# A new order for the prologue of a fused vision-transformer block, and for the first image's gates and weight mixing in its feed-forward phase

## The reference, cut to what matters

```python
h = tok(x, W, b, cls)                       # (4, 3137, 128)
h = h + attn(layernorm(h), ...)
h = h + ffn(layernorm(h), ...)
# attn: q, k, v = causal 4-tap convolutions of linear maps, silu, q and k normalised
#   S_t = a_t (S - b_t (S k_t) k_t^T) + b_t v_t k_t^T ;  o_t = S_t q_t
#   out = linear(zero-centred rms norm(o) * silu(linear(x)))
# ffn: gh = relu(x W^T + b) ; g = (gh gfc2^T + b2).mean(tokens)     # 8 gates per image
#   W1m = W1 + sum_e g_e tv_W1[e] ; W2m = W2 + sum_e g_e tv_W2[e]   # b1m, b2m alike
#   out = layernorm(x + relu(x W1m^T + b1m) W2m^T + b2m) * lng + lnb
```

## Time and profile before

| | |
|---|---|
| median of 3 runs | 855.02 us (854.75 to 856.34) |
| the profiled execution: time, span | 857.75 us, 855.8 us |
| mean granted TensorE clock | 0.992 |
| TensorE, VectorE, ScalarE, GpSimd busy | 95%, 76%, 58%, 43% of the span |
| instructions | 31627 |

### The profile page before, as it was taken

One profiled execution on the slowest core, in us unless ns is written; L12 is line 12 of the kernel. 1 busy time (PEld: TensorE's weight loads), 2 busy tenths in 40 slices (PEclk: granted clock), 3 DMA queues, 4 the chain that ended last, 5 costly groups with the idle time before them and its releaser, 6 DMA issues. The chain is left out here.

```text
span 855.8 us, 31627 instructions
## 1 busy us (share of the span) xinstructions
PE 817.1 (95%) x12064; PEld 643.9 (75%) x12064; DVE 646.8 (76%) x2313; ACT 500.3 (58%) x1773; POOL 364.8 (43%) x530
## 2 busy tenths in 40 slices
PE   7679999999999999999999999999999899999996
PEld 5457778787787788787787787777787577777775
DVE  4356888888888888888888888888784867777444
ACT  1335566666565666666665666666645366666664
POOL 3122332333333332333323333333311388888875
PEclk9989999999999999999999999999999999999999
DMA  2000122221122111111101111111012133333331
GB/s 59 16 12 13 47 61 50 62 62 50 45 58 54 33 32 31 38 38 34 36 25 38 33 25 37 38 32 32 28 53 74 34 113 119 118 112 111 111 111 44
DMA packets 78660, 45.35 MB, mean 53 GB/s; under 512 B 20357, under 2 KB 69803, under 8 KB 78511
## 3 DMA queue, kind: packets, MB, share of 16 engines
q1 hardware_dynamic: 77663, 42.80, 17.9%
q10 hardware_dynamic: 848, 0.54, 0.3%
HBM read 23.69 MB, written 19.63 MB: 51 GB/s over the span
## 5 line engine op out<-in xcount | busy, mean ns | idle before, releaser
L1952 ACT ACTIVATE work<-bank,b1mix 128x512 f32<-128x512 f32 x96 | 66.0, 688 | 63.5 <-PE bank L2047 63.4
L2073 PEld LDWEIGHTS bank<-work 128*128 128x128 f32 x768 | 89.7, 192 | 11.8 <-issue 11.8
L2047 PE MATMUL bank<-work 128*128 128x512 f32 x192 | 88.3, 602 | 3.2 <-DVE work L1827 3.2
L2073 PE MATMUL bank<-work 128*128 128x128 f32 x768 | 89.6, 275 | 0.0
L491 ACT ACTIVATE work<-bank 128x512 f32<-128x512 f32 x50 | 29.9, 598 | 98.3 <-PE bank L1330 98.3
L740 POOL TENSOR_SCALAR var2e<-mv 128x4 f32<-128x4 f32 x22 | 5.0, 229 | 167.0 <-DVE mv L946 167.0
L1329 PE MATMUL bank<-SA,work 128*128 128x256 f32 x200 | 69.5, 430 | 0.0
L2047 PEld LDWEIGHTS bank<-work 128*128 128x128 f32 x192 | 35.1, 193 | 38.7 <-issue 34.5
L1330 PE MATMUL bank<-SB,work 128*128 128x256 f32 x200 | 61.1, 388 | 0.0
L1280 PEld LDWEIGHTS bank<-work 32*32 32x32 f32 x3200 | 35.1, 107 | 32.9 <-issue 27.3
L1869 DVE TENSOR_TENSOR work<-bank,work 128x512 f32<-128x512 f32 x24 | 16.6, 692 | 55.6 <-PE bank L2073 55.6
(11 more groups left out here) (288 smaller groups left out, 2373.3 us busy)
## 6 DMA issues: line engine op xcount, KB each, us to landing
hn_kept<-work SPq DMA_DIRECT2D x25, 256.0 KB, 2.5
hnT_kept<-work SPq DMA_DIRECT2D x25, 256.0 KB, 2.3
work<-hnT_kept SPq DMA_DIRECT2D x25, 256.0 KB, 2.8
work<-hn_kept SPq DMA_DIRECT2D x25, 256.0 KB, 3.1
out_dram<-work SPq DMA_DIRECT2D x24, 256.0 KB, 2.5
tv<-in_L_ffn_tv_W_dram SPq DMA_DIRECT2D x16, 256.0 KB
work<-r_kept SPq DMA_DIRECT2D x25, 98.0 KB
work<-in_x_dram SPq DMA_DIRECT2D x23, 102.0 KB
```

Of the source, the lines that this page charges most:

```text
L1952: ins = nc.scalar.activation(hid[f][:, :], ps[:, :], ACT.Relu, bias=b1mix[:, of[0], f:f + 1])
L2047: ins = mm(ps[:, :], w1T[of[0]][:, f, :], ghT[par][:, :, :].rearrange("p t c -> p (t c)"), start=True, stop=True)
L2073: ins = mm(by4(bank[2 + par])[:, t, :], hid[f][:, t * C:(t + 1) * C], w2T[of[t]][:, f, :], start=(f == 0 and t == 0), stop=(f == FB - 1), ...
```

## The change

In the first pass the embedding now stands ahead of all constant products: it is followed by the transpose of the centred weights, the three tap products and four products of ones (`transpose_weights`), then the factor's transpose, then the folding products and twelve products of ones. VectorE copies the folded weights between statistics and their aggregation, does the output weights and masks and the folding in other places, with a last part (`fold_rest`) behind the pixel product. ScalarE's copies of the taps and gates follow the factor row. The thirteen loads follow the row's loads. In the second pass the factor row and the key columns come ahead of the queries, the query rows go to the end, with six products of ones behind them. The third pass gets products of ones at four places. In the feed-forward phase the first image's gates are made first, with a release of their own, the others' after four mixing steps; GpSimd's shift of the residual goes ahead, its bias additions go behind the last mixing step; the b2 products go between the first two and last two hidden products of the first unit. The helper functions in the second pass hold the code that stood there before; where they are only moved, the diff below leaves them out.

```diff
-        WARM = 8
+        WARM = 11
...
-            ffn["load"](sp)
...
+                if j == first:
+                    ffn["load"](sp)
...
-            act.wait_ge(taps_ps, 1)
-            for t, i in ((cwA, 0), (cwB, 4), (cbs, 2)):
-                ins = nc.scalar.copy(t, bank[i][:, 0:384])
-            ins.then_inc(taps_kept, 1)
-            act.wait_ge(gate_ps, 1)
-            nc.scalar.copy(SA[0:64, 256:386], bank[6][0:64, 0:130]).then_inc(gate_kept, 1)
+
+            def folded_parts():
+                act.wait_ge(taps_ps, 1)
+                for t, i in ((cwA, 0), (cwB, 4), (cbs, 2)):
+                    ins = nc.scalar.copy(t, bank[i][:, 0:384])
+                ins.then_inc(taps_kept, 1)
+                act.wait_ge(gate_ps, 1)
+                nc.scalar.copy(SA[0:64, 256:386], bank[6][0:64, 0:130]).then_inc(gate_kept, 1)
...
+                fill = j == first + 1
+                if fill:
+                    factor_row()
+                    keys_out()
+                    key_squares_and_queries()
+                else:
+                    key_squares_and_queries()
+                    factor_row()
+                    if j == first:
+                        folded_parts()
+                    query_squares()
+                    keys_out()
...
+                if fill:
+                    query_squares()
...
+                ffn["scalar_early"](act)
...
-                dve.wait_ge(pro_dve, 3)
+
+            def fold_rest():
+                kv, q = bank[5][:, 0:256], bank[5][:, 256:384]
+                dve.wait_ge(pro_dve, 4)
                 nc.vector.tensor_tensor(SA[:, 0:256], cbs[:, 0:256], SA[:, 0:256], ALU.add)
                 nc.vector.tensor_tensor(SB[:, 0:256], cwB[:, 0:256], kv, ALU.mult)
-                dve.wait_ge(pro_dve, 4)
+                dve.wait_ge(pro_dve, 5)
                 nc.vector.tensor_tensor(SA[:, 386:514], cbs[:, 256:384], SA[:, 386:514], ALU.add)
                 nc.vector.tensor_tensor(SB[:, 384:512], cwB[:, 256:384], q, ALU.mult).then_inc(folded, 1)
...
-                dve.wait_ge(pro_dve, 5)
+                dve.wait_ge(pro_dve, 3)
...
                     ins.then_inc(stats1_done, 1)
                     if s > 0:
                         keep_h0()
+                    else:
+                        fold_weights()
                     dve.wait_ge(stats1_done, s + 1)
                     need(dve, var1e_ready, s)
                     for b in range(NB):
                         ins = nc.vector.bn_aggr(mv1[:, b, :], stats1[:, b, :])
                     ins.then_inc(mv1_ready, 1)
                     if s == 0:
-                        fold_weights()
                         keep_h0()
-                        fold_taps()
                         output_weights()
...
+                if j != first + 1:
+                    key_factors()
...
+                if j == first + 1:
+                    key_factors()
...
                 if j == first:
-                    sub_masks()
+                    fold_taps()
...
+                if j == first:
+                    fold_rest()
+                    sub_masks()
...
-            pe.wait_ge(con, 2)
-            pe.wait_ge(taps_in, 16 * len(conv_taps))
-            mm(bank[0][:, 0:384], selA, cwT, start=True, stop=True)
-            mm(bank[4][:, 0:384], selB, cwT, start=True, stop=True)
-            mm(bank[2][:, 0:384], onehot1, cb_row[:, 0:384], start=True, stop=True).then_inc(taps_ps, 1)
             pe.wait_ge(we_in, 16 * len(embedding))
 
-            def fold_weights():
+            def keep_busy(n, at=7):
+
+                for _ in range(n):
+                    mm(bank[at][:, 0:D], ones[:, :], ones[:, :], start=True, stop=True)
+
+            def transpose_weights():
+                pe.wait_ge(con, 2)
                 pe.wait_ge(zeroed, 1)
                 pe.wait_ge(Wc_ready, 1)
                 tr(bank[3][:, 0:D], Wc, ident[:, :]).then_inc(WcT_ps, 1)
+                pe.wait_ge(taps_in, 16 * len(conv_taps))
+                mm(bank[0][:, 0:384], selA, cwT, start=True, stop=True)
+                mm(bank[4][:, 0:384], selB, cwT, start=True, stop=True)
+                mm(bank[2][:, 0:384], onehot1, cb_row[:, 0:384], start=True, stop=True).then_inc(taps_ps, 1)
+                keep_busy(4)
+
+            def fold_weights():
                 pe.wait_ge(WcT_ready, 1)
                 pe.wait_ge(proj_in, 16 * len(projection))
                 for to, at, n in ((0, 0, 256), (256, 384, 128)):
@@ -1261,6 +1304,8 @@
                     mm(bank[6][:, to:to + n], WcT, rhs_all[:, at:at + n], start=True, stop=False)
                     ins = mm(bank[6][:, to:to + n], onehot2, bias_row[:, at:at + n], start=False, stop=True)
                 ins.then_inc(gate_ps, 1)
+                pe.wait_ge(r_row_ready, 1)
+                keep_busy(12)
 
...
+                        if j == first + 2:
+                            pe.wait_ge(ssq_ready, 1)
...
                 if j == first:
-                    fold_weights()
+                    transpose_weights()
...
+                elif I_:
+                    keep_busy(3, 6)
...
+                elif I_:
+                    keep_busy(4, 6)
...
+                if fill:
+                    pe.wait_ge(kvg_ready, KV_PARTS * s1 + 1)
+                    factor_row()
+                    key_columns()
+                    queries()
+                    alpha_rows()
+                else:
+                    queries()
+                    factor_row()
+                if j == first:
+                    fold_weights()
...
+                elif I_:
+                    keep_busy(4, 6)
...
+                if not fill:
+                    query_rows()
...
+                elif I_:
+                    keep_busy(3, 6)
+                if not fill:
+                    key_columns()
...
+                if not fill:
+                    alpha_rows()
...
+                if fill:
+                    query_rows()
+                    keep_busy(6, 6)
...
-        nc.vector.scalar_tensor_tensor(g_all[:, :, :], bank[0][:, 0:NB * NE].rearrange("p (b e) -> p b e", b=NB), 1.0 / TOK,
-                                       gfc2b[:, :].unsqueeze(1).broadcast_to([D, NB, NE]), ALU.mult, ALU.add)
+        nc.vector.scalar_tensor_tensor(g_all[:, 0, :], bank[0][:, 0:NE], 1.0 / TOK, gfc2b[:, :], ALU.mult, ALU.add)
         nc.vector.tensor_scalar(g_T[0:NE, :], bank[0][0:NE, 64:64 + NB], 1.0 / TOK, gfc2b_col[:, :], ALU.mult, ALU.add).then_inc(g_ready, 1)
         dve.wait_ge(g_ready, 1)
-        for k in range(NE):
+        for k in range(NE // 2):
+            mix0(k)
+        dve.wait_ge(g_ps2, 2)
+        nc.vector.scalar_tensor_tensor(g_all[:, 1:NB, :], bank[7][:, 0:(NB - 1) * NE].rearrange("p (b e) -> p b e", b=NB - 1), 1.0 / TOK,
+                                       gfc2b[:, :].unsqueeze(1).broadcast_to([D, NB - 1, NE]), ALU.mult, ALU.add).then_inc(g_ready, 1)
+        for k in range(NE // 2, NE):
             mix0(k)
         dve.wait_ge(b1_ps, 1)
         nc.vector.tensor_tensor(b1mix[:, :, :], bank[6][:, 0:NB * FB].rearrange("p (f b) -> p b f", b=NB),
                                 b1nat[:, :].unsqueeze(1).broadcast_to([D, NB, FB]), ALU.add).then_inc(b1_ready, 1)
         for k in range(NE, 3 * NE):
             mix0(k)
+        dve.wait_ge(g_ready, 2)
...
-    def scalar(act):
-
+    def scalar_early(act):
         act.wait_ge(ln_ps, 1)
         nc.scalar.copy(lng_lnb[:, :, :], bank[5][:, 0:2 * D].rearrange("p (a c) -> p a c", a=2)).then_inc(ln_ready, 1)
+
+    def scalar(act):
+
         act.wait_ge(A["wo_ps"], STEPS)
...
+        pool.wait_ge(ln_ready, 1)
+        shift_h1(0)
         pool.wait_ge(b2_ready, 1)
-        pool.wait_ge(ln_ready, 1)
+        pool.wait_ge(mix0_step, 3 * NE)
         biased(0)
-        shift_h1(0)
         biased(1)
...
         pe.wait_ge(gh_ready, 1)
-        for b in range(NB):
-
-            mm(bank[0][:, b * NE:(b + 1) * NE], gh[:, b:b + 1].broadcast_to([D, D]), gfc2T[:, :], start=True, stop=True)
+        mm(bank[0][:, 0:NE], gh[:, 0:1].broadcast_to([D, D]), gfc2T[:, :], start=True, stop=True)
         mm(bank[0][0:NE, 64:64 + NB], gfc2T[:, :], gh[:, :], start=True, stop=True).then_inc(g_ps2, 1)
+        for b in range(1, NB):
+            ins = mm(bank[7][:, (b - 1) * NE:b * NE], gh[:, b:b + 1].broadcast_to([D, D]), gfc2T[:, :], start=True, stop=True)
+        ins.then_inc(g_ps2, 1)
...
-        for b in range(NB):
-            ins = mm(by4(bank[7])[:, b, :], g_T[:, b:b + 1].broadcast_to([NE + 1, D]), tvb2[:, :], start=True, stop=True)
-        ins.then_inc(b2_ps, 1)
-
         pe.wait_ge(ln_ready, 1)
+
+        def biases2():
+            pe.wait_ge(g_ready, 2)
+            for b in range(NB):
+                ins = mm(by4(bank[7])[:, b, :], g_T[:, b:b + 1].broadcast_to([NE + 1, D]), tvb2[:, :], start=True, stop=True)
+            ins.then_inc(b2_ps, 1)
...
             for f in range(FB):
+                if u == 0 and f == HALF:
```

(24 more changed lines are left out.)

122 lines of the change are left out of this document (57 added, 65 removed).

## The result

The changed kernel takes **846.13 us** (median of 4 runs, 845.34 to 848.14) against 855.45 beside it: a ratio of 0.9894, 95% interval 0.9873 to 0.9915. That is faster, as forecast, but by 9.3 us and not 19, and 846.13 lies 0.1 us beyond the forecast's range. The profiled execution took 845.34 us with a span of 843.3, so profile against profile the gain is 855.8 - 843.3 = 12.5 us.

A forecast was written before the change was run, and what follows sets the result against it. It took the serial first 27 us, TensorE's low clock and slow feed-forward mixing as bounds; 9.3 + 3.5 + 2.3 - 0.5 + 4.4 = 19.0 us saved gave 836.0 us for the median, range 831 to 846.

The forecast's parts named there:

- the prologue's term: Up to the first gate products: start at 17.5 us, not 26.84, saving 9.3 us; bounds nothing and 10.5.
- rival A: The forecast itself: TensorE's clock is up by the tap products and stays; 832 to 839 us, chance 0.50.
- Rival B: Prologue: clock stays low until the twelve fillers or key products; first term 0 to 5, 840 to 845 us, chance 0.25.
- The additions' lock: Last normalisation beside GpSimd's moved shift of the residual: counted at 0, bound 1.26 us, the price of one addition.
- rival C: GpSimd's additions lock out VectorE at their new places, normalisation waits 1.26 us; 837 to 839 us, chance 0.12.
- The second step: From 26.84 to 44.69 us: half of 7.0 us at the low clock comes back, 3.5 us; bounds 0 and 5.
- the third: Third step, from 44.69 us: higher clock less exposed fillers saves 2.3 us; bounds -3.8 and 3.2.
- The loads' collision: Moved feed-forward loads could delay the second row's round trip by nothing to 2 us; charged 0.5.
- The feed-forward start: Gates, weight mixing and second hidden pair: earlier gates, unlocked mixes, faster pair save 4.4 us; bounds 2.5 and 5.
- Rival D: Fillers in TensorE's queue in the first three steps cost time at the low clock: slower, 860 us, chance 0.06.
- Rival E: First stage bound by something the order does not touch, above all the first tile's pixels; 854 to 856 us, chance 0.07.

The follow-up runs named there:

- b1_rows128_shift: Changed kernel with tap and bias products on 128 zero-padded rows and the residual's first shift held until the last normalisation is done: 837.47 us.
- c2_before_rows128: Kernel of before with only the tap and bias products padded to 128 rows with zeros: 851.26 us.
- c4_loads_early: b1_rows128_shift with the 13 feed-forward loads back ahead of the step loop, as in the kernel of before: 838.5 us.
- a1_ffn_only: Kernel of before with the new feed-forward phase alone: 852.5 us.
- b3_taps128: Changed kernel with only the four-row tap products on 128 zero-padded rows, bias products left at one row: 841.79 us.
- c1_fill_one_row: b1_rows128_shift with the twelve fillers behind the folding made over 1 row in place of 128: 841.05 us.
- c3_warm8: b1_rows128_shift with eight warm-up products in place of eleven: 840.63 us.
- a2_rows128: Changed kernel with tap and bias products on 128 zero-padded rows: 841.29 us.

## Why the prediction was wrong, step by step

**The step that failed** is in the prologue's term: the folding products counted at half (3.1 us) and the twelve fillers at 3.2, which is the second half of rival A, "the clock is up by the tap products and stays". It was up by the tap products, and did not stay: it fell at 10.2 us, the folding took 6.1 and the fillers 5.5, and the term measured 3.7 and not 9.3. Its working was right otherwise: with the rows padded the same order starts the gate products at 16.53 (b1_rows128_shift), a first term of 26.84 - 16.53 = 10.3, inside the bound of 10.5, and the kernel takes 837.5, inside the 832 to 839 of A. Of the 6.65 us between the two profiles' gate products, 2.8 are the slow folding, behind which VectorE's and ScalarE's steps ended at 18.8 and not at 16.0, and the rest the fillers. The evidence stood in the prediction as "against" A: two stretches of 6.2 us, "nearly unbroken", that "did not raise" the clock. They are the tap and the folding products; I read them as a reason to doubt and not for what they have in common, products over 4 rows and over 1 row (the earlier trace rows shows the first). A term that took them so would have had the clock falling behind the tap products. But the rows are not the whole reason why those two stretches did not raise the clock: in c2_before_rows128 they didn't with 128 rows either, and why stays open.

**Rival B** priced the term at 0 to 5, which holds the measured 3.7, but its course was wrong: it has the clock low from the start, when it rose, fell and rose again behind the twelve fillers. That its number fits is luck.

**The additions' lock** was counted at 0 and cost 1.06 us, near the 1.26 given as its bound, so rival C's lock came true as well. The rivals were priced apart, and the range's far end, which adds one lock to B's 845, was set 0.1 us too low. The Trainium skill (SBUF — State Buffer, Who interferes with whom) names a scalar operation with one tile operand among those that can enter a two-port mode, and says that whichever engine issues first holds the shared pair for its whole instruction. The trace agrees with that reading and not with the one I took: the normalisation lost 2.17 - 1.11 = 1.06 us to one addition of 1.26. Which mode it ran in, no row shows.

**The second step** gave 3.4 (forecast 3.5) and **the third** 1.9 (2.3). In the second the gate and key products, at the high level now, account for 2.9 of it (7.9 us from 26.84 before, 5.0 from 23.18 now); the rest is not taken apart. **The loads' collision** with the second row, charged at 0.5, did not occur: that row leaves at 29.08 and its reload is issued at 30.27, the same 1.19 us as the first row's. By c4_loads_early's timeline the move even gained 0.5 us on the way of the first factor row. **The feed-forward start** gave 4.4, as forecast, and a1_ffn_only has the same 15.17 us from the gates to the second group with the old prologue, the lock of 1.06 apart; some 0.9 of the 4.4 was the low clock of the second hidden pair in the one profile of before (c2_before_rows128).

**Rival D** (fillers on the path) happened in small: from 18.8 to 23.2, 4.4 us of the twelve stood on the path, and the other terms outweighed them. **Rival E** did not happen: the embedding product starts between 5.7 and 6.2 us in every profile of the new order, as forecast.

**From the profile to the median** the prediction subtracted the same saving. Gains that come from the clock are not the same in every execution: the runs of before beside the last eight experiments range from 853.2 to 857.8 us with mean granted clocks of 0.978 to 0.993, and the profile that the prediction was worked from took 857.75. Against the median 3.2 of the 12.5 us are not there; the low clock of that profile's third step and second hidden pair, which c2_before_rows128's profile did not have, goes the same way.

## What to carry to other kernels

Work that is there to keep TensorE's clock up, or that fills a gap in front of work that needs it, should use all 128 rows. Here products over 1 and 4 rows cost at least the same time and let the clock fall, so pad such products with zeros where they stand ahead of a critical stretch and the clock is up (4.8 us by medians, 846.1 to 841.3, the clock and the alternation of rows together). Row counts in between were not varied. A filler's worth depends on where the clock stands: the same twelve products were worth 2.9 us where it was up, and stood 4.4 us on the path where it had fallen; the three added warm-up products, before it had first risen, were worth 3.2. When an elementwise step moves to GpSimd's free time, look at what VectorE does at that moment, also where VectorE's instruction has one tile operand: one wait on the idle engine gave back 1.06 us on the critical one, and 2.3 where TensorE's clock fell behind the lock.

## What the runs showed that was not expected

- At the high level, products over 1 row that alternate with products over 128 rows follow each other at 0.42 us (128 columns, b3_taps128), where products over 128 rows follow at 0.22. In TensorE's timeline, b3_taps128 and then b1_rows128_shift:

```profile
12.08 0.48 PE L1304 MATMUL bank<-work 1*128 1x128 f32 x2
12.49 0.49 PE L1307 MATMUL bank<-work 128*128 128x128 f32 x2
```

```profile
11.93 0.39 PE L1306 MATMUL bank<-work 128*128 128x128 f32 x2
12.16 0.39 PE L1309 MATMUL bank<-work 128*128 128x128 f32 x2
```

  The whole folding takes 3.4 us (10.51 to 13.95) and 2.2 (10.78 to 12.97); at the low level 6.2 in the kernel of before and 4.3 in c2_before_rows128. So 1.2 to 1.9 us of the padding's gain is not the clock's. In c1_fill_one_row, where one-row products follow each other, they cost no more than full ones.
- The granted clock can fall while TensorE is busy without a break (10.2 us in the changed kernel, 14.9 in b3_taps128).
- Its column reads 1.00 until the first change is recorded, as in the earlier trace rows: in c3_warm8 it shows 1.00 from the start, over embedding products of 2.04 us. So a 1.00 ahead of the first change has to be confirmed by durations.
- The same pause was followed by a fall of the clock in some profiles and not in others: behind the lock in a2_rows128 and b3_taps128 and not in the changed kernel, and behind the end of the second step in four of eleven.
